# A fused attention and feed-forward layer on eight cores: the second feed-forward matrix is staged in other buffers, the second block takes feed-forward work from its first step, and the other matmuls go in pieces of four

## The reference

```python
x = x + attn(layernorm(x))          # x: 16 x 2048 x 1024, f32
x = x + ffn(layernorm(x))

def attn(x):                        # 16 query heads of 64, 4 groups of keys and values
    xn = layernorm(x) * ln_scale + ln_bias
    q, (k, v) = xn @ Wq, split(xn @ Wkv)        # Wq 1024x1024, Wkv 1024x512
    q, k = layernorm(q), layernorm(k)           # over each head's 64, with scale and bias
    p = softmax(q @ k.T / 8)                    # per head, 2048 keys
    return (p @ v) @ Wout                       # Wout 1024x1024

def ffn(x):                         # weights to -s, 0, s; activations to 8 bits per row
    h = gelu(quant(x) @ ternary(w1).T)          # w1 4096x1024
    return quant(h) @ ternary(w2).T             # w2 1024x4096
# ternary(w): s = mean|w|, round(w/s) clipped to -1..1, times s
```

## Time and profile before

| | |
|---|---|
| time, median of 3 runs | 2154.29 us (2152.71 to 2158.37) |
| the profiled execution's own time | 2159.15 us |
| its span (slowest core, core 7) | 2157.6 us |
| spans of the 8 cores | 2144.6 to 2157.6 us |
| busy: TensorE, ScalarE, VectorE | 1869.8, 1416.3, 1201.2 us |
| block 1, from one write of AO to the next | 402.4 to 643.8 us |
| blocks 2 and 3 likewise | 643.8 to 871.05, 871.05 to 1092.1 us |

### The profile page before, as it was taken

One profiled execution on the slowest core, in us unless ns is written; L12 is line 12 of the kernel. 1 busy time (PEld: TensorE's weight loads), 2 busy tenths in 40 slices (PEclk: granted clock), 3 DMA queues, 4 the chain that ended last, 5 costly groups with the idle time before them and its releaser, 6 DMA issues.

```text
span 2157.6 us, 42477 instructions; the slowest of 8 cores (2144.6 to 2157.6 us)
## 1 busy us (share of the span) xinstructions
PE 1869.8 (87%) x16196; PEld 891.9 (41%) x16196; DVE 1201.2 (56%) x1725; ACT 1416.3 (66%) x1466; POOL 127.7 (6%) x109
## 2 busy tenths in 40 slices
PE   3645667667999999999999999999999999998897
PEld 2213333333444444444444444444445444444343
DVE  5445888775535554464556446554555545445663
ACT  6457767556677777777777777777777787773120
POOL 0420012100000100010000000000000000000000
PEclk9777789778999999999999999999999999999999
DMA  9499754550322232423233322332233232222412
GB/s 295 125 304 336 260 185 157 176 166 17 69 64 58 79 77 45 95 82 94 45 74 103 94 45 69 108 92 48 69 108 89 45 74 55 50 45 69 98 39 69
DMA packets 235142, 225.27 MB, mean 104 GB/s; under 512 B 203328, under 2 KB 203584, under 8 KB 227136
## 3 DMA queue, kind: packets, MB, share of 16 engines
q1 hardware_dynamic: 234944, 222.56, 37.8%
HBM read 135.51 MB, written 36.70 MB: 80 GB/s over the span
## 4 chain that ended last, share of the span: by engine, by line
PE 61%; ACT 12%; DVE 12%; issue 10%; DMA 4%; POOL 1%; SPq 1%; DVEq 0%; ACTq 0%; POOLq 0%
PE PA L875 16%; PE PA L886 14%; PE PS L779 9%; PE PV L795 9%; ACT P L921 6%; PE PA L846 4%; PE PA L865 4%; DMA X<-x 3%; PE PA L819 2%; ACT H L929 2%; ACT L931 1%; DVE s_tmp L1244 1%; DVE HQ L1260 1%; ACT HQ L951 1%; ACT L926 1%
## 5 line engine op out<-in xcount | busy, mean ns | idle before, releaser
L921 ACT ACTIVATE P<-PS,s_nbnd 128x1024 bf16<-128x1024 f32 x1024 | 1078.1, 1113 | 395.8 <-PE PS L779 395.5
L875 PE MATMUL PA<-W,YB 128*128 128x512 fp8e4 x2048 | 484.9, 382 | 11.8 <-DVE H L1237 7.6
L886 PE MATMUL PA<-W,HT 128*128 128x512 fp8e4 x1984 | 459.8, 379 | 0.0
L779 PE MATMUL PS<-QB,K 64*128 64x512 bf16 x2048 | 337.7, 393 | 108.7 <-ACT P L921 106.3
L795 PEld LDWEIGHTS PV<-V,P 128*128 128x128 bf16 x8192 | 304.9, 99 | 196.1 <-issue 142.9
L795 PE MATMUL PV<-V,P 128*128 128x65 bf16 x8192 | 344.7, 196 | 37.1 <-DVE AO L1078 37.1
L1237 DVE TENSOR_SCALAR H<-PA,s_c 128x512 f32<-128x512 f32 x256 | 190.7, 749 | 329.5 <-PE PA L875 329.4
L875 PEld LDWEIGHTS PA<-W,YB 128*128 128x128 bf16 x2048 | 184.8, 98 | 244.3 <-issue 57.5
L886 PEld LDWEIGHTS PA<-W,HT 128*128 128x128 bf16 x1984 | 180.4, 98 | 220.4 <-issue 29.4
L779 PEld LDWEIGHTS PS<-QB,K 64*128 64x128 bf16 x2048 | 71.9, 94 | 276.4 <-issue 263.9
L929 ACT ACTIVATE H<-H 128x2048 f32<-128x2048 f32 x64 | 118.7, 1902 | 71.8 <-DVE H L1237 71.6
(11 more groups left out here) (120 smaller groups left out, 1198.0 us busy)
## 6 DMA issues: line engine op xcount, KB each, us to landing
X<-x SPq DMA_DIRECT2D x56, 512.0 KB, 5.2
W<-w1t SPq DMA_DIRECT2D x18, 1024.0 KB, 11.8
y<-X SPq DMA_DIRECT2D x32, 512.0 KB, 3.1
H<-w2t SPq DMA_DIRECT2D x14, 1024.0 KB, 11.0
WR<-scr_wo SPq DMA_DIRECT2D x6, 2048.0 KB, 8.1
W<-w2t SPq DMA_DIRECT2D x10, 1024.0 KB, 22.0
WR<-scr_wq SPq DMA_DIRECT2D x5, 2048.0 KB, 9.7
H<-w1t SPq DMA_DIRECT2D x8, 1024.0 KB, 15.6
```

What stands on the lines that cost most here:

```text
L779: ins = q.matmul(out=PS[:, i % 2, 512 * r:512 * r + 512], lhsT=K[64 * r:64 * r + 64, s, pr, 128 * kt:128 * kt + 128], rhs=QBc[p % 2][64 * ...
L875: ins = q.matmul(out=o, lhsT=YT[:, c], rhs=W1[:, c, 512 * n:512 * n + 512], start=(c == 0), stop=(c == 7))
L886: ins = q.matmul(out=o, lhsT=HTc[T == NT - 1][:, c], rhs=W2[:, c, 512 * h:512 * h + 512], start=(c == 0), stop=(c == 31))
L921: q.activation(out=P[:, i % 4], in_=PS[:, i % 2], func=AF.Exp, bias=nbnd[:, 0:1], scale=0.125).then_inc(sems["EXP"], 1)
```

## The change

1. **Staging of w2.** SH becomes five buffers that take nothing of H or HQ: HT, three quarters of the W2 tile's own space that are written late (the former SG 3, 2, 1), and the upper half of X2. `SH_SLOT` gives each piece its buffer and `SH_PUT` the step of its load. F1E waits for WT 0, 11 only; the first HTD waits for WT 1, 15; the loads of x for tiles 2 and 3 (LX, into the half of X2) wait for WT 1, 14 and stand behind it in the plan. When each WT is put is unchanged.
2. **Feed-forward from step 0 of block 1.** `FIRST` and the marker are gone, `STAGE` has an entry `1: 0`. Block 1 begins with LX, LAO, a gap of 4.0, WO 0, WO 1, then F1 of tile 0 with the Q of block 2 laid in it, Wq loaded before (WRQ 1), Wout after (WRO 1). Wout is first loaded at the end of block 0 (WRO 0). The same tiles fall in the same blocks.
3. **Pieces of four.** KV, Q, WO, F1 and F2 are laid in pieces of 4 matmuls at cost 1.0, where they were of 8 at 2.0. Instructions, waits and their order within a set are the same.

```diff
-STAGE = {2: 4, 3: 8, 4: 12, 5: 16, 6: 20}
-FIRST = 24
+STAGE = {1: 0, 2: 4, 3: 8, 4: 12, 5: 16, 6: 20}
+SH_SLOT = (0, 1, 2, 3, 0, 1, 2, 4, 0, 1, 4, 0, 4, 0, 4, 0)
+SH_PUT = {55: (0,), 57: (1, 2, 3), 58: (4,), 59: (5,), 60: (6,), 61: (7,), 62: (8,), 63: (9,), 65: (10,), 66: (11,),
+          68: (12,), 69: (13,), 70: (14,), 71: (15,)}
...
     def F1(T):
-        return [(2.0, f1, T, n) for n in range(8)]
+        return [(1.0, f1, T, n, k) for n in range(8) for k in (0, 1)]
     def F2(T):
-        return [(2.0, f2, T, h, k) for h in (0, 1) for k in range(4)]
+        return [(1.0, f2, T, h, k) for h in (0, 1) for k in range(8)]
...
-        if 55 <= i < 71:
-            put("sp", "SH", i - 55)
+        for r in SH_PUT.get(i, ()):
+            put("sp", "SH", r)
+        if i == 72:
+            put("sp", "LX", 2)
+            put("sp", "LX", 3)
...
-        if p < 2:
-            jobs += [(0.0, put, "sp", "LXT", p + 1)]
-            jobs += Q(A) + [(0.6, kt, 7)] * (p == 0) + Q(A + 1) + [(0.6, qt, A)] + Q(A + 2) + [(0.6, qt, A + 1)] + Q(A + 3)
-            jobs += [(0.6, qt, A + 2), (0.6, qt, A + 3)]
-            if p == 1:
-                jobs += [(0.0, put, "sp", "WRO", 1), (0.0, lao, 0), (0.0, lao, 1)]
-                jobs += [(0.0, put, "sp", "LX", t) for t in range(4)]
-                jobs += [(0.0, None)]
+        if p == 0:
+            jobs += [(0.0, put, "sp", "LXT", 1)]
+            jobs += Q(A) + [(0.6, kt, 7)] + Q(A + 1) + [(0.6, qt, A)] + Q(A + 2) + [(0.6, qt, A + 1)] + Q(A + 3)
+            jobs += [(0.0, put, "sp", "WRO", 0), (0.6, qt, A + 2), (0.6, qt, A + 3)]
+        if p == 1:
+            jobs += [(0.0, put, "sp", "LX", 0), (0.0, put, "sp", "LX", 1), (0.0, lao, 0), (0.0, lao, 1), gap(4.0)]
...
-                    jobs += F1(T)[:6] + Q(A) + F1(T)[6:] + Q(A + 1) + F2(T - 1)[:4]
+                    first, second = (F2(T - 1)[:8], F2(T - 1)[8:]) if T else ([gap(6.0)], [gap(4.0)])
+                    jobs += F1(T)[:12] + Q(A) + F1(T)[12:] + Q(A + 1) + first
                     jobs += [(0.0, ytd, T + 1), (0.6, qt, A)] + Q(A + 2) + [(0.6, qt, A + 1)] + Q(A + 3)
-                    jobs += [(0.0, put, "sp", "WRO", p)] + F2(T - 1)[4:]
+                    jobs += [(0.0, put, "sp", "WRO", p)] + second
                     jobs += [(0.6, qt, A + 2), (0.6, qt, A + 3), (0.0, lao, T + 2)]
...
-            if hold and k == FIRST:
-                jobs.pop(hold[0])
-                base, granted = then, spent
...
-    SH = [SG[4], SG[5], HQ.bitcast(F32), HT.bitcast(F32)]
+    SH = [HT.bitcast(F32), SG[3], SG[2], SG[1], X2[:, 2:4].rearrange("p k w -> p (k w)")]
...
             elif kind == "SH":
-                if r >= 4:
-                    sp.wait_ge("WT", 1, r - 4)
-                elif r < 2:
-                    sp.wait_ge("WT", 0, 10 + r)
+                was = [k for k in range(r) if SH_SLOT[k] == SH_SLOT[r]]
+                if was:
+                    sp.wait_ge("WT", 1, was[-1])
...
             elif kind == "F1E":
-                dve.wait_ge("WT", 1, 15)
+                dve.wait_ge("WT", 0, 11)
```

More of the change, by code:

```diff
@@ L118, in xt, with kv @@
         put("act" if b < 4 else "dve", "XTE", b, j)
-    def kv(T):
-        put("pe", "KV", T)
+    def kv(T, k=None):
+        if k != 1:
+            put("pe", "KV", T)
+        if k == 0:
+            return
+        pl.order["pe"].append(("KV+", T))
         put("act", "KVE", T)
@@ L143, in kt, with q @@
         put("dve", "KTE", b)
[L145 to L148, removed]
+    def q(T, h, k=None):
+        if k != 1:
+            if T >= 2:
+                pl.need("QN", T - 2)
+            put("pe", "Q", T, h)
+        if k == 0:
+            return
+        pl.order["pe"].append(("Q+", T, h))
         put("dve", "QE", T, h)
@@ L162, in lao, with wo @@
         put("sp", "LAO", T)
[L164 to L168, removed]
+    def wo(T, h, k):
+        if k == 0:
+            pl.need("LX", T)
+            if T and h == 0:
+                pl.need("YQ", T - 1)
+            put("pe", "WO", T, h)
+            return
+        pl.order["pe"].append(("WO+", T, h))
         put("dve", "WOE", T, h)
@@ L177, in ytd, with f1 @@
         put("sp", "YTD", T)
[L179 to L182, removed]
+    def f1(T, n, k):
+        if k == 0:
+            if T and n == 0:
+                pl.need("HQ", T - 1, 1)
+            put("pe", "F1", T, n)
+            return
+        pl.order["pe"].append(("F1+", T, n))
         put("dve", "F1E", T, n)
@@ L473, in make_plan @@
                             put("sp", "AOS", kt2 // 128)
-            while pos < len(jobs) and jobs[pos][1] and (last or spent + jobs[pos][0] / 2 < granted):
+            while pos < len(jobs) and (last or spent + jobs[pos][0] / 2 < granted):
                 cost, fn, *args = jobs[pos]
@@ L809, in _ @@
                 ins.then_inc(sems["XT"], 1)
[L810 removed]
+            elif kind in ("KV", "KV+"):
                 T, = ix
                 b, t = divmod(T, 4)
[L813 to L815 removed]
+                first = kind == "KV"
+                if first:
+                    free("KV", T)
+                    pe.wait_ge("XTE", b, 3)
+                    pe.wait_ge("WKC", 1)
                 o = bank(F32, "KV", T)
                 xn = XT[b]
[L818 removed]
+                for c in range(4) if first else range(4, 8):
                     ins = q.matmul(out=o, lhsT=xn[:, c, 128 * t:128 * t + 128], rhs=WKV[:, c],
                                    start=(c == 0), stop=(c == 7))
[L821 removed]
+                if not first:
+                    ins.then_inc(sems["KV"], 1)
             elif kind == "KT":
@@ L857, in _ @@
                 ins.then_inc(sems["QT"], 1)
-            elif kind == "WO":
+            elif kind in ("WO", "WO+"):
                 T, h = ix
-                free("WO", T, h)
-                pe.wait_ge("LAO", T)
-                pe.wait_ge("WRO", stages(T) - 1)
+                first = kind == "WO"
+                if first:
+                    free("WO", T, h)
+                    pe.wait_ge("LAO", T)
+                    pe.wait_ge("WRO", stages(T) - 1)
                 o = bank(F32, "WO", T, h)
-                for c in range(8):
+                for c in range(4) if first else range(4, 8):
                     ins = q.matmul(out=o, lhsT=AOT[:, T % 2, c], rhs=WRc[:, c, 512 * h:512 * h + 512],
                                    start=(c == 0), stop=(c == 7))
-                ins.then_inc(sems["WO"], 1)
-            elif kind == "F1":
+                if not first:
+                    ins.then_inc(sems["WO"], 1)
+            elif kind in ("F1", "F1+"):
                 T, n = ix
-                free("F1", T, n)
-                pe.wait_ge("YTD", T)
-                pe.wait_ge("WT", 0, 15)
+                first = kind == "F1"
+                if first:
+                    free("F1", T, n)
+                    pe.wait_ge("YTD", T)
+                    pe.wait_ge("WT", 0, 15)
                 o = bank(F32, "F1", T, n)
-                for c in range(8):
+                for c in range(4) if first else range(4, 8):
                     ins = q.matmul(out=o, lhsT=YT[:, c], rhs=W1[:, c, 512 * n:512 * n + 512],
                                    start=(c == 0), stop=(c == 7))
-                ins.then_inc(sems["F1"], 1)
+                if not first:
+                    ins.then_inc(sems["F1"], 1)
             elif kind in ("F2", "F2+"):
```

88 lines of the change are left out of this document (44 added, 44 removed).

## The result

The changed kernel takes 2141.02 us (median of 5 runs, 2138.29 the fastest), the kernel before 2157.97 on the same chip: a ratio of 0.993 [0.9916, 0.9944]. The forecast was 2144. The profiled execution took 2141.02 us, the span of its slowest core, 2, is 2139.5.

A forecast was written before the change was run, and what follows sets the result against it. VectorE was taken to bound block 1's first part, TensorE's columns later blocks. 2159.15 - 7.7 (block 1) - 2 (pieces) = 2149.4; that execution being 4.9 above the median gave 2144.6, stated as 2144, range 2119 to 2163.

The forecast's parts named there:

- Block 1, 7.7 us less: Block 1, from one AO write to the next: 233.7 us against 241.4 before, 7.7 us less.
- 18 us from AOS to the first WOE: Head of block 1: 12.5 us until LAO lands, then 5.7 to the end of the first WOE, about 18.
- 88.7 us for VectorE's 79.8 at 0.9: Block 1, rest of steps 0 to 22: VectorE has 79.8 us left and is busy 0.9, so 88.7 us.
- 127 us for the second part: Block 1, steps 23 to 63: 119 us, plus 3 to the next AOS and 5 for clock and rest, 127.
- Staging elsewhere: New w2 staging loads: costed at nothing, or 2 us a piece for two or three pieces if loads collide.
- A late WO delays SH loads behind it: SyncE's queue: Wq and Wout loads wait for WO and Q, delaying later SH loads; covered by the 0.9.
- Pieces of four, 2 us less in blocks 2 to 7: Blocks 2 to 7: S waits shrink 5 us, more changes of work cost 3; net 2 us less.
- the forecast's 28 us: TensorE, blocks 2 to 7: by the skill's rule, 280 more pieces at 0.1 us a load would add 28 us.
- Rival 1: Block 1's first part: VectorE does not hold it; block 205 us, 36 less, total 2116; chance 0.12.
- Rival 2: Blocks 2 to 7: even pieces empty the waits, 33 us less there, total 2114; chance 0.06.
- Rival 3: Block 1: ScalarE's small operations queue behind WT, 10 to 17 us more, total 2162 to 2169; chance 0.16.
- Rival 4: Block 1: nothing moved that counts, early gains are waited away at LAO and the first gelu; 2154; chance 0.06.

The follow-up runs named there:

- the order: Changed kernel with AO written in four transfers and the transposed loads queued ahead of LX 0, LX 1 and a w2 load: 2130.93 us, ratio 0.99.
- the lighter WT: Changed kernel with the second of WT's two VectorE operations left out for the last twelve pieces of w2: 2125.32 us, ratio 0.9859.

## Why the prediction came out right, point by point

That the total came out right is luck: of its terms one was too good by some 19 us, another left out 18.8 us, and the two cancelled. By the medians over cores:

- **Block 1, 7.7 us less.** It was 2.9 (7.8 between the slowest cores). From AOS to AOS in the traced core it is 239.1 us, forecast 233.7. *18 us from AOS to the first WOE*: 19.9 (397.82 to 417.68), a stop of 12.87 us. The size was nearly right, its reason half: the two transfers do follow each other, but AOS takes 8.9 us and not 5.8, for the bytes ahead of it. Taking the wait for AOS away brought 1.0 us, the order 5.8, both together 9.8. *88.7 us for VectorE's 79.8 at 0.9*: the window 417:497 has VectorE 73.65 of 80 (0.92), and the last WT ends 99.3 us after AOS where 106.7 was forecast; VectorE had 6 us less to do than I added up (and the addition itself gives 79.3, not 79.8). That it is the fuller engine is shown by the lighter WT, that it isn't the only one too. *127 us for the second part*: 139.8 from 497.12 to the next AOS at 636.93. This is the mis-sized term. 5 us of it are where AOS falls, 8 us into block 2 and not 3. The rest is waits: TensorE waits 14.5 us in 497:629, 7.0 of it for exponentials, and the clock of 0.97 takes 4; I had 11.4 for both.
- **Staging at nothing.** Shown wrong for the staging alone (19.7 us, from the queue). In the whole change Q doesn't follow the head of the block, and what is left of the cost is probably in the stop; it wasn't timed by itself there. "A late WO delays SH loads behind it" had the direction the wrong way round: the SH loads held what others needed.
- **Pieces of four, 2 us less in blocks 2 to 7.** It was 7.9 (7.1 with the pieces only). And with the pieces only block 0 had 5.0 less and block 1 13.8, for which I had written nothing. The step that failed is the one that looked for the pieces' worth only at gelu steps: where TensorE and VectorE wait for each other, smaller portions take most of the waits away (13.4 us to 2.6, 8.7 to 0.6), and that is in blocks 0 and 1. The price of a change between attention and other work, put at 0.01 us, holds. TensorE in block 3 of the changed kernel:

```profile
957.47 1.03 PE L864 MATMUL PA<-WR,QB 128*128 128x512 bf16 x4
958.43 0.60 PE L792 MATMUL PS<-QB,K 64*128 64x512 bf16 x4
958.97 1.04 PE L911 MATMUL PA<-W,HT 128*128 128x512 fp8e4 x4
959.84 0.65 PE L808 MATMUL PV<-V,P 128*128 128x65 bf16 x16
```

  Four matmuls take 0.96 us before an S and 0.87 before a PV: 0.865 + 0.09 and 0.865, as with eights. The rule of the Trainium skill ("TensorE: Matmul & The Clock Gate", Part 3), by which a weight load overlaps running matmuls only in another row group, doesn't show here. What speaks against it is the pace within a run, 0.216 us a matmul with a weight load for each. The pieces are no test of it, and the forecast's 28 us don't follow from it: both kernels have 16196 matmuls and as many loads, so by the rule every one would pay, in pieces of any size.
- **Rival 1** (VectorE doesn't hold the first part) fell: its first part would be under 90 us, and it is 99; that VectorE isn't alone in holding it was half of it. **Rival 2** took place by a quarter: 7.9 of 33 us, block 3 at 219.6, and the S still wait 3.3 us. **Rival 3** fell: VectorE was 0.92 busy, above the 0.83 at which it decides, though R3 waits 8.3 us for VectorE in 398:497. **Rival 4** (what is won at first is lost later) is nearest to what early feed-forward does: 19.1 us more in steps 0 to 22 and 18.3 less behind them, and then the stop on top. It predicted no change for the whole because it gave the pieces next to nothing.

So three terms made the sum: pieces in blocks 0 and 1 (18.8 us by the pieces-only kernel, forecast 0), pieces later (7 to 8, forecast 2), and early feed-forward with the new staging (11 the other way, forecast 7.7 less). The last one is what the change was made for, and its sign was wrong.

Open: what limits the WT part once VectorE is relieved wasn't followed to its end, and why moved feed-forward work costs in steps 0 to 22 just what it saves later is argued from the clock (0.89 against 0.97) and VectorE's share, not shown. With pieces of four the planner also puts each job at another point of its step, and no run parts that from the size of the portion.

## What to carry to other kernels

Where two engines pass work through a shallow buffer, try half the portion first: it cost nothing here and was worth 1.2%, where the restructuring beside it lost time. Before a load is moved, read the queue in which it will stand, for the waits ahead of it and the bytes ahead of it: two loads queued behind a late wait cost 18 us, the bytes in front of a transpose 6. When a change has several parts, time them apart, since a total that agrees with the forecast can be two errors that cancel.

## What the runs showed of the hardware

- A DMA transpose that waits for nothing landed in 11.1 us behind 3 MB of other transfers, in 5.6 to 6.3 ahead of them, and in 4.0 to 5.5 where the kernel before issues it. 3 MB at the 279 GB/s of that stretch are 11 us, so the bytes ahead explain most of it.
- While TensorE stands in this stop the granted clock is 0.50, 1.2 GHz, and the four matmuls after it take 1.87 us against 1.03 at 957.47.
- Changing TensorE from a run of 128-row matmuls to a PV costs nothing that the trace shows (runs of 4 and 16), and to an S 0.09 us (runs of 4 and 8).
